# Attention rows in float16: moving their transposes from TensorE and ScalarE to DMA

## The reference

```python
# 1. 4 x 1024 tokens of 256 features: RMS norm, short convolution and gating, MLP with relu
# 2. mixture of experts: 32 experts, 6 a token, plus a shared expert
# 3. layernorm, attention, layernorm, FFN, layernorm:
q, k, v = x @ w_q.T, x @ w_k.T, x @ w_v.T       # 16 heads of 16
q, k = rope(q), rope(k)
s = q @ k.T / 4                                  # per head
o = softmax(s, where block(key) <= block(query)) @ v   # blocks of 64 tokens
x = layernorm(x + o @ w_o.T)
h = silu(x @ w_gate) * (x @ w_up)
h = the 2 of every 4 entries of h that are largest in magnitude, the others 0
x = layernorm(x + h @ w_down)
```

## Time and profile before

| | |
|---|---|
| median of 3 runs | 1815.63 us (1812.99 to 1818.59) |
| profiled execution, first to last instruction | 1811.6 us |
| attention and FFN phase | from about 687 us to the end |
| one batch (heads stage and FFN stage) | 265 us; heads 113 to 117 of them |
| busy share of the span | PE 85%, DVE 64%, ACT 45%, POOL 13% |

### The profile page before, as it was taken

The page is one execution under the profiler, slowest core; times in us unless marked ns, Lnnn a source line. Parts: engine busy times, 40 slices in busy tenths (PEclk is TensorE's granted clock), DMA queues, the critical chain, the costliest instruction groups (busy, mean ns, idle before and its releaser), DMA issues.

```text
span 1811.6 us, 27446 instructions
## 1 busy us (share of the span) xinstructions
PE 1542.5 (85%) x10490; PEld 961.8 (53%) x10491; DVE 1153.6 (64%) x2399; ACT 822.2 (45%) x1352; POOL 234.8 (13%) x237
## 2 busy tenths in 40 slices
PE   3999999977989973589888989888989888989796
PEld 2899988864568772233344534254534344433355
DVE  5566666637421145678568778668778678778475
ACT  5444444512212213347855157744157753177530
POOL 5334444412400001000000000100000100000000
PEclk8999999978999986669999989989999999989999
DMA  2000000105215502000000000000000000000000
GB/s 107 12 25 24 23 23 24 34 12 174 51 37 148 153 1 96 1 1 2 1 1 1 0 1 1 25 1 1 1 1 1 24 1 1 1 1 2 24 1 24
DMA packets 27153, 48.04 MB, mean 27 GB/s; under 512 B 7312, under 2 KB 16016, under 8 KB 26256
## 3 DMA queue, kind: packets, MB, share of 16 engines
q1 hardware_dynamic: 26464, 44.74, 7.7%
q0 software_dynamic: 576, 1.77, 0.4%
HBM read 37.59 MB, written 9.06 MB: 26 GB/s over the span
## 4 chain that ended last, share of the span: by engine, by line
issue 60%; POOL 2%; DVE 0%; POOLq 0%; DVEq 0%
POOL rs_sb L1340 1%; POOL ve_sb L1337 0%; POOL qks_sb L1355 0%; POOL v_sb L1354 0%; POOL qks_sb L1345 0%; DVE bn_sb L1545 0%; DVE x_sb_sb L1560 0%; POOLq L1159 0%; POOLq L65 0%; POOL qks_sb L1356 0%; DVE mv_sb L1551 0%; DVEq L1159 0%; POOL v_sb L1353 0%; DVE ident_h_sb L1742 0%; DVEq L65 0%
## 5 line engine op out<-in xcount | busy, mean ns | idle before, releaser
L1612 DVE TENSOR_REDUCE mx_sb<-s_ps 128x1 f32<-128x512 f32 (+1 forms) x512 | 312.8, 652 | 111.9 <-PE s_ps L1906 65.0
L1418 ACT ACTIVATE room_sb<-s_ps 128x1024 f32<-128x1024 f32 (+1 forms) x320 | 283.5, 949 | 23.7 <-PE s_ps L1930 22.5
L1903 PE MATMUL s_ps<-room_sb 48*128 48x512 f16 (+3 forms) x640 | 177.1, 343 | 39.9 <-DVE mx_sb L1607 20.0
L1903 PEld LDWEIGHTS s_ps<-room_sb 48*128 48x128 f16 x640 | 52.9, 96 | 210.3 <-DVE mx_sb L1612 126.4
L1930 PE MATMUL s_ps<-room_sb 51*128 51x128 f16 (+4 forms) x1152 | 145.3, 283 | 22.3 <-ACT room_sb L1418 14.9
L1950 PE MATMUL cm_ps<-room_sb,v_sb 128*32 128x512 f32 (+3 forms) x1536 | 162.3, 511 | 0.8 <-ACT room_sb L1424 0.8
L1337 POOL TENSOR_TENSOR ve_sb<-mv_sb,eps_sb 128x4 f32<-128x4 f32 x24 | 5.0, 210 | 1081.5 <-DVE mv_sb L1551 1081.5
L2072 PE MATMUL cm_ps<-w_fd_sb,room_sb 128*128 128x256 f32 x512 | 131.4, 406 | 14.7 <-DVE room_sb L1694 14.7
L394 DVE SCALAR_TENSOR_TENSOR x_sb_sb<-xp_sb,conv_w_sb,x_sb_sb 128x512 f32<-128x512 f32 x96 | 109.2, 1139 | 22.6 <-ACT x_sb_sb L319 20.5
L2072 PEld LDWEIGHTS cm_ps<-w_fd_sb,room_sb 128*128 128x128 f32 x512 | 97.3, 198 | 38.4 <-issue 14.0
L2059 PE MATMUL s_ps<-xbT_sb,w_fg_sb 128*128 128x512 f16 x384 | 100.3, 391 | 10.2 <-DVE ctok_sb L1660 8.7
(11 more groups left out here) (255 smaller groups left out, 3194.6 us busy)
## 6 DMA issues: line engine op xcount, KB each, us to landing
we_gu_sb<-we_gu SPq DMA_DIRECT2D x32, 352.0 KB
we_dn_sb<-we_dn SPq DMA_DIRECT2D x32, 176.0 KB
x_in_sb<-x SPq DMA_DIRECT2D x9, 512.0 KB, 3.5
rows<-x_sb_sb SPq DMA_DIRECT2D x8, 512.0 KB, 3.0
x_sb_sb<-rows SPq DMA_DIRECT2D x2, 2048.0 KB, 12.0
out<-x_sb_sb SPq DMA_DIRECT2D x8, 512.0 KB, 2.6
xp_sb<-w_in SPq DMA_DIRECT2D x1, 1024.0 KB, 5.7
x_sb_sb<-w_up SPq DMA_DIRECT2D x1, 1024.0 KB, 7.3
```

Of the source, the lines that this page charges most:

```text
L1418: act.activation(weights[(g * NU + u) % SLOTS_P][:, 2 * pair:2 * pair + 2, 0:width(u) * P], W[s % 2][:, :, 0:width(u) * P], ACT.Exp, scale ...
L1612: dve.tensor_reduce(mx[:, pair, k % 2, slot:slot + 1], X[:, k % 2, 0:count * P], AX.X, ALU.max, negate=True).then_inc(mx_ok, 1)
L1903: last = pe.matmul(X[:, k % 2, at * P:(at + plain) * P], query[head:head + NORM, i * P:(i + 1) * P], key[head:head + NORM, j * P:(j + plai ...
```

## The change

SyncE issues DMAs that transpose while they copy (`dma_start_transpose`): `x_turned` for each tile (128x512 float16), `turned_rows` for k and q of each group and pair (128x1024 each), `q_max_turned` for q with maxima of groups 1 to 3. Only group 0's q with maxima is still turned by TensorE and copied by ScalarE. `qks` is laid out so that the rows of a pair lie together; `w_qk` is stored without the grouping; ScalarE and VectorE write the same numbers of elements. `AHEAD` goes from 6 to 8, the six maxima ahead of step 0 are gone, and the first 8 steps of group 0 hold three each. The two semaphores for loaded constants are one, so VectorE waits for the FFN's weights too before it writes the mask.

```diff
-AHEAD = 6
+AHEAD = 8
...
+            if g == 0 and s < AHEAD:
+                return ((1, 3 * s, 3 * s + 3),)
+            low = AHEAD + 2 * s
+            return ((g + 1, low, low + 2),) if low < 2 * NX else ((g + 2, low - 2 * NX, low - 2 * NX + 2),)
...
         @block.sync
...
+            def x_turned(c, t):
+                k = c * ST + t
+                wait(sync, xs_low, k + 1)
+                wait(sync, qkv_mm, k - 1)
+                sync.dma_start_transpose(xt[:, t % 2, :, :, :].rearrange("p a f c -> p (a f) c"),
+                                         xs[:, t % 2, :, :].rearrange("p a c -> p (a c)")).then_inc(xt_in[t % 2], 16)
+            def turned_rows(b, g, pair):
+                n = b * NHG + g
+                before = n - (3 if pair == 0 and g == 3 else 2)
+                if g == 0:
+                    wait(sync, sc_mm, STEPS * n)
+                elif g == 3 or (g, pair) == (2, 1):
+                    wait(sync, sc_mm, STEPS * (before + 1))
+                wait(sync, qk_in[pair], 32 * n)
+                for tiles, s in ((kT, 1), (qT, 0)):
+                    sync.dma_start_transpose(of_pair(tiles, g, pair).rearrange("p (t c) -> p t c", t=ST),
+                                             rows_of(g, s, pair)).then_inc(qk_in[pair], 16)
+            def q_max_turned(b, g, pair):
+                wait(sync, nm_ok, group(b, g)(2, LEAD + pair + 1))
+                q_max_landed(sync, b, g, pair, 1)
+                sync.dma_start_transpose(of_pair(qT, g, pair).rearrange("p (t c) -> p t c", t=ST),
+                                         rows_of(g, 0, pair)).then_inc(qmT, 16)
...
+            for b in range(NB):
+                for t in range(ST):
+                    x_turned(b, t)
+                wait(sync, ca_ok, (b + 1) * ST)
+                wait(sync, low_ok, (b + 1) * ST)
+                wait(sync, zeroed, b + 1)
...
+                for pair in range(2):
+                    turned_rows(b, 0, pair)
+                wait(sync, hs_ok, 4 * b)
+                turned_rows(b, 1, 0)
+                turned_rows(b, 1, 1)
+                turned_rows(b, 2, 0)
+                for g in range(1, NHG):
+                    q_max_turned(b, g, 0)
+                    q_max_turned(b, g, 1)
+                    if g == 1:
+                        turned_rows(b, 2, 1)
+                        turned_rows(b, 3, 0)
+                    if g == 2:
+                        turned_rows(b, 3, 1)
+                if b > 0:
+                    stored(b - 1)
...
             def x_high(c, t):
-                wait(act, tx, k - 1)
+                if k > 1:
+                    xt_landed(act, k - 2)
...
             def heads(b):
                 scores(b, 0, 0)
-                qk_transposed(b, 1, 0, 1)
-                wait(pe, qm_ok, group(b, 0)(2, 1))
-                qk_transposed(b, 1, 0, 0)
-                for_maxima(b, 1, 0, AHEAD)
-                q_max_transposed(b, 0, 1)
+                q_max_transposed(b, 1)
...
-                        if g + 1 < NHG:
-                            if s == 3:
...
-                                qk_transposed(b, g + 1, 1, 1)
-                            if s == 5:
...
-                                qk_transposed(b, g + 1, 1, 0)
-                            if s == 11:
...
-                                q_max_transposed(b, g + 1, 0)
-                        if g + 2 < NHG:
-                            if s == 13:
...
-                                qk_transposed(b, g + 2, 0, 1)
-                            if s == 15:
...
-                                qk_transposed(b, g + 2, 0, 0)
```

255 lines of the change are left out of this document (85 added, 170 removed).

## The result

The changed kernel takes 1833.4 us (median of 5 runs, 1830.4 to 1843.1); the kernel before, beside it, 1818.6 (5 runs, 1813.0 to 1821.4). The ratio is 1.0085, 95% interval 1.0049 to 1.0121: slower by 0.85%, about 15 us, where 34 us less was forecast. The profiled execution of the changed kernel took 1841.1 us, 7.6 above its median, with a span of 1839.2; so its difference from the profile before (27.6 us of span) is larger than the 15 us between the medians, and what follows is read from a run of the changed kernel that is longer than most.

What follows compares the result with a forecast made beforehand. It took the loop of maxima in the heads stages as the bound. Savings of 25.0 us (heads), 5.7 (FFN) and 3.5 (start) summed to 34.2, giving a median of 1781.4 us; forecast range 1760 to 1805, over all 1752 to 1850.

Steps and rivals of the forecast that it cites:

- What bounds the kernel: Middle of the heads stages: the loop of maxima is the bound, not TensorE and not ScalarE.
- loop of maxima: Heads stages: TensorE at most two maxima ahead of VectorE's reductions; two steps take 3.3 us with or without transposes.
- The transposes lie in its shadow: Middle of heads stages: a set of eight is worth 0, at most 0.62 us; 1.0 per batch taken for all.
- L: Time of a transposing DMA: taken as 4.1 us for 256 KB and 3.4 for 128 KB, range 2.6 to 10.4.
- slow-transfer rival: Scores wait for slow transfers at changes of group; at 10.4 us a transfer the kernel takes 1865; chance 0.28.
- Beginning of a heads stage: Start of each batch's heads stage: scores of step 1 come 3.8 us sooner, 2.2 saved; 4.0 in the first batch.
- Changes of group: Heads stages: transposes and waits gone at two changes, 1.7 us per batch; 0.9 more at the end of group 2.
- FFN stages: The three FFN stages with qkv in them: 1.9 us saved in each, 5.7 in all.
- Before the first heads stage: Backlog between the last qkv and the row transposes goes: 3.5 us saved.
- tile loop: Before the first heads stage: with DMA it runs over two tiles, 5.1 us a tile; last qkv hardly earlier.

Runs made afterwards that it cites:

- e1: Kernel after, plus 8 unread TensorE transposes of the identity at each old transpose place of the heads stages (filler); 1826.9 us, ratio 1.0023 to the kernel before.
- e10: Kernel after with the two waits the filler needed, but no filler; 1835.5 us, ratio 1.0070 to the kernel before.
- the square: Ratios to the kernel before: three maxima a step 1.0085 without filler, 1.0023 with; six ahead, two a step 0.9977 without, 0.9917 with.
- e2: Kernel before, one transpose in place of eight for rows of groups 1 to 3 in batches 1 to 3, no transposing DMA; 1819.4 us, ratio 0.9989.
- e3: Kernel after with the old order at a batch's start (six maxima ahead, then two a step); 1819.5 us, ratio 0.9977 to the kernel before.
- e6: Kernel after with the edits of e1 and e3 together (filler and old order); 1804.7 us, ratio 0.9917 to the kernel before.
- e4: Kernel after with each of the 64 transposing DMAs for rows of q and k done twice; 1835.4 us, ratio 1.0068 to the kernel before.
- e8: Kernel before with x transposed by DMA in all four batches, rows of q and k as before; 1812.5 us, ratio 0.9962.
- e5: Kernel before with x transposed by DMA in the first batch alone; 1810.6 us, ratio 0.9949.
- e9: e6 with the six fillers of a group at steps 3, 6, 8, 11, 14, 17 in place of 3, 5, 11, 13, 15, 19; 1816.3 us, ratio 0.9966.
- e7: e6 with filler in the FFN stages as well, where x and group 0's rows were transposed; 1809.1 us, ratio 0.9940 to the kernel before.

## Why the prediction was wrong

The sign was wrong. By its own steps:

- **What bounds the kernel: right, and the reason for the loss.** The loop of maxima takes 3.31 us at full clock with and without transposes. The step that failed is the one behind it: "The transposes lie in its shadow", priced at "worth 0; its upper bound is 0.62" and never below nothing. What lay in the shadow was also load. Without it the clock fell in the groups with maxima, and a round of two steps took 4.81 us at the lower clock in place of 3.31; unread transposes at the same places brought groups 1 and 2 back to full clock, 8 of 8 against 5 of 24, and 0.0062 of the time. The rows for this were there: the prediction gave the clock of 0.97 and named it "the 2.4 GHz level", but kept it as a constant of the kernel. Of each term it should have asked what the clock does. Shown by e1 against e10 (filler against its waits alone), and by the square; in the kernel before by e2, in groups 0 and 2. The transposes are not all that this clock hangs on: the old order alone (e3) kept 6 of the 8 groups at full clock, and with filler on it (e6) it was 4.
- **L: mis-sized on the safe side.** Taken 4.1 and 3.4, measured 3.3 and 2.5. The slow-transfer rival had the sign and not the mechanism: e4 excludes it. The Trainium skill's page DMA: Bandwidth & Descriptors, with 261 GB/s for transposes and 2.0 us of fixed time, gave an estimated 3.0 us, near the measured 3.3 (the page gives the 2.0 for DMAs that GpSimd issues; these are issued by SyncE); the estimate of 10.5 us from VectorE: DVE Perf Modes, with 1309 ns a block taken one after the other, was wrong here.
- **Beginning of a heads stage: forecast 2.2 us a batch (4.0 in the first), a loss in its place.** Part of it came as computed: in the third batch the scores of step 1 come 3.6 us behind those of step 0 (1328.82 to 1332.43; forecast 4, before 7.8). But from the scores of step 0 to the exponential of step 10 it is 27.1 us after and 23.1 before. I had counted three maxima a step from VectorE's reductions, as if TensorE kept up. These two windows, before and after, show the clock at 0.85 and 0.55 and TensorE nearly 5 us longer busy:

```profile
1321.62:1344.70 23.08, 17.51 (x173) 7.50 (x173) 16.89 (x34) 15.20 (x17) 0.00 (x0) 0.85 0.00 1
```

```profile
1328.82:1356.00 27.18, 22.23 (x145) 7.60 (x145) 18.65 (x37) 11.12 (x13) 0.00 (x0) 0.55 0.05 10
```

With the old order and the filler the FFN stage and group 0 together are 184.0 us a batch against 186.7 before (552.0 and 560.2 in three batches). No run has three maxima a step at full clock, so how much of its 0.0107 is the clock and how much the order itself stays open.
- **Changes of group: 1.7 + 0.9 forecast.** The DMA wait at the change to group 3 was 0.73 and 0.80 us, forecast about 1; the other changes have none. But group 1 as a whole won nothing: at full clock and without filler it took 30.8 us in the third batch of e10, against 30.4 before; group 2 took 28.1 in the first batch after and 29.1 before. So the middle and the changes were worth about 0.6 a batch there, and 1.1 with the old order (e3: 29.86 and 28.53), not 3.6: mis-sized, also without the clock.
- **FFN stages: 5.7 forecast, nothing came.** e8 is not faster than e5 (0.9962 and 0.9949), and two of three stages are 1.4 and 0.6 us longer, the third 6.5, at a lower clock (0.89 against 0.94). Whether the 1.9 us a stage would come at an unchanged clock no run shows.
- **Before the first heads stage: 3.5 forecast, 10 to 13 came.** The forecast let the tile loop win nothing ("the last `qkv` ends hardly earlier"). A tile took 3.7 to 4.4 us in place of up to 7.06; the estimate of 5.1 a tile had `qkv` at 1.2 GHz (4.2 us), while it ran at the upper level (1.47 + 0.82). From the end of the last `qkv` to the first maximum it is 10.8 us after and 13.2 before, 2.4 less, where 3.5 was forecast. Here the clock helped: the prologue's mean from first `qkv` to first maximum rose from 0.69 to 0.88 in these two profiles, but in e9, whose code is the same there, it was 0.70 and the stretch 43.6 us, so some 10 us are the DMA's own.

Timeline of PE, the last three tiles and the first maximum after; beside the earlier trace rows, the 2.61 us of waiting for the split are 1.6 to 2.2 for the DMA:

```profile
726.59 1.47 PE L1878 MATMUL s_ps<-w_qk_sb,xt_sb 128*128 128x512 f16 x6 [1.73 <-DMA xt_sb<-xs_sb]
...
730.31 1.47 PE L1878 MATMUL s_ps<-w_qk_sb,xt_sb 128*128 128x512 f16 x6 [1.60 <-DMA xt_sb<-xs_sb]
...
734.68 1.47 PE L1878 MATMUL s_ps<-w_qk_sb,xt_sb 128*128 128x512 f16 x6 [2.24 <-DMA xt_sb<-xs_sb]
...
747.63 0.40 PE L1905 MATMUL s_ps<-room_sb 51*128 51x128 f16 x4 [10.83 <-DMA room_sb<-qks_sb]
```

What stays open: which of the places of the filler is needed (4 to 8 transposes, with or without the start, can't be told apart by their times), why e6 had fewer of groups 1 and 2 at full clock than e3, why e7's FFN filler brings nothing although e8's FFN stages ran at a lower clock, the share of the order itself, and why the order at the start of a batch changes the clock of the groups behind it.

## What to carry to other kernels

Before work is taken from TensorE's idle time, ask what its granted clock stands on: a transpose that costs nothing is also load, and when the clock falls without it everything else on TensorE is slower. Read the mean clock before and after together with the span, then by window; fewer instructions with more busy time is its mark. If it fell, unread work at the places where TensorE waits anyway brings it back (here 0.6%), while the same work where TensorE is waited for costs most of its length (0.5 of 0.62 us in e9). Ask the same of the order of the work: here it weighed more than the transposes (1.1%).

## What was not expected of the hardware

- The time of one and the same program follows the clock: of 35 runs of the kernel before on one chip, nine runs at a mean clock of 0.920 or less took 1829.4 us on average, five at 0.928 or more 1814.6. That is the scatter under every comparison here, and why a single profile can't price a change of 0.5%.
- The Trainium skill's page TensorE: Matmul & The Clock Gate, Part 4: PE-mode transpose, says that the upper clock doesn't engage for a transpose. Here the trace disagrees: with 8 transposes of the identity at a place (0.62 us) groups 1 and 2 were at the upper level in 8 of 8 cases (e1), with the same waits and none in 3 of 8 (e10). They stood among other matmuls; no run shows transposes alone.
- The same code reached its first `qkv` at 706 to 708 us in some profiles and at 711 to 715 in others, in which the stretches at the lower clock before it lie elsewhere.
- A transposing DMA of 256 KB within SBUF took 3.3 us from issue to landing (3.1 to 5.1), one of 128 KB 2.5, and SyncE about 1.2 us each to issue; with twice as many of the larger ones for k and q the kernel took the same time (e4).
